# Three normalisations per half step: split in SBUF and turned by DMA instead of TensorE, two PSUM rings, the A and C layers swapped, and the loops written out

## What is computed

```
x = x + 0.5 * ffn(layernorm(x))          # layer A
x = x + ssm(layernorm(x))                # layer B (the names of the reference call it attention)
x = x + 0.5 * ffn(layernorm(x))          # layer C, the same weights as A

ffn: h = silu(x @ wg.T) * (x @ wu.T); h @ wd.T          # 256 -> 768 -> 256, int weights / 127
ssm: x_in, z = split(x @ in_w.T)                        # 256 -> 2 x 512
     xc = causal conv of 4 taps over x_in + bias
     dt_r, Bm = xc @ x_proj.T;  delta = clip(softplus(dt_r @ dt_w.T + dt_b), 0.001, 0.1)
     h = scan over tokens of exp(delta*A) * h + (exp(delta*A) - 1) / A * Bm      # 128 states
     out = ((h @ C.T + xc * D) * silu(z)) @ out_w.T
```

## Time and profile before

| what | us |
|---|---|
| median of three runs | 574.49 |
| lowest and highest run | 569.34, 575.93 |
| the profiled execution | 570.68 |
| its span | 568.8 |
| PE busy | 511.2 (90%) |
| DVE busy | 439.5 (77%) |

### The profile page before, as it was taken

The page is one execution under the profiler, slowest core; times in us unless marked ns, Lnnn a source line. Parts: engine busy times, 40 slices in busy tenths (PEclk is TensorE's granted clock), DMA queues, the critical chain, the costliest instruction groups (busy, mean ns, idle before and its releaser), DMA issues.

```text
span 568.8 us, 8689 instructions
## 1 busy us (share of the span) xinstructions
PE 511.2 (90%) x2705; PEld 297.9 (52%) x2705; DVE 439.5 (77%) x896; ACT 263.9 (46%) x449; POOL 227.5 (40%) x192
## 2 busy tenths in 40 slices
PE   3779978989999899888999899988999899998776
PEld 3346426636484357535484366535485366645434
DVE  5886897898768975798768986698868985797442
ACT  5374642456416471356506562355605563356032
POOL 2320246163623726053532817144441827153323
PEclk9969979999999999999999999999999999999979
DMA  9301000000200010000200011000200000000101
GB/s 303 89 1 39 2 0 2 0 2 3 75 2 1 1 61 17 3 2 2 75 2 1 1 39 39 3 2 1 76 2 1 1 20 21 1 1 3 37 1 38
DMA packets 14577, 13.80 MB, mean 24 GB/s; under 512 B 2592, under 2 KB 13856, under 8 KB 14512
## 3 DMA queue, kind: packets, MB, share of 16 engines
q1 hardware_dynamic: 13696, 12.12, 6.9%
q10 hardware_dynamic: 816, 0.79, 0.4%
HBM read 8.71 MB, written 4.19 MB: 23 GB/s over the span
## 4 chain that ended last, share of the span: by engine, by line
PE 31%; issue 30%; POOL 18%; DVE 17%; ACT 2%; DMA 1%; POOLq 1%; DVEq 0%; ACTq 0%
PE q L1259 17%; PE dp L1259 10%; POOL hl L418 6%; POOL xcl L425 4%; POOL yu L433 4%; DVE xn L706 3%; DVE h L728 3%; PE tp L1170 2%; DVE xc L756 2%; POOL rs_A L404 1%; POOL rs_C L404 1%; DVE yu L822 1%; DMA xpre<-in_L_attn_x_dram 1%; PE q L1170 1%; DVE xl L715 1%
## 5 line engine op out<-in xcount | busy, mean ns | idle before, releaser
L418 POOL TENSOR_TENSOR hl<-h,hh 128x512 f16<-128x512 f32 x96 | 119.2, 1249 | 111.1 <-ACT hh L548 110.1
L756 DVE SCALAR_TENSOR_TENSOR xc<-xi,cw,xc 128x512 f32<-128x512 f32 x96 | 93.5, 974 | 2.9
L728 DVE SCALAR_TENSOR_TENSOR h<-sg,hsm,q 128x512 f32<-128x512 f32 x96 | 70.7, 742 | 27.1 <-PE q L1259 14.4
L425 POOL TENSOR_TENSOR xcl<-xc,xch 128x512 f16<-128x512 f32 x32 | 43.9, 1383 | 90.2 <-ACT xch L563 90.2
L548 ACT ACTIVATE hh<-h 128x512 f16<-128x512 f32 x96 | 60.0, 625 | 42.1 <-DVE h L728 41.5
L533 ACT ACTIVATE xh<-tp 128x512 f16<-128x512 f32 x48 | 25.9, 592 | 114.5 <-PE tp L1170 114.1
L1259 PE MATMUL q<-xh,wu 128*128 128x512 f16 x192 | 57.8, 383 | 21.2 <-DVE h L728 19.3
L544 ACT ACTIVATE sg<-q 128x512 f32<-128x512 f32 x96 | 56.6, 589 | 28.3 <-PE q L1259 28.3
L1259 PE MATMUL dp<-wo,yu 128*128 128x256 f32 x256 | 58.6, 381 | 1.5 <-POOL yu L433 1.5
L1259 PE MATMUL q<-xh,wg 128*128 128x512 f16 x192 | 57.5, 381 | 2.6 <-DVE xl L715 2.0
L1259 PE MATMUL q<-xl,wg 128*128 128x512 f16 x192 | 57.8, 382 | 0.0
(11 more groups left out here) (177 smaller groups left out, 772.6 us busy)
## 6 DMA issues: line engine op xcount, KB each, us to landing
xpre<-in_L_attn_x_dram SPq DMA_DIRECT2D x8, 512.0 KB, 4.3
out_dram<-x SPq DMA_DIRECT2D x16, 256.0 KB, 2.2
xc<-in_L_attn_in_proj_w_dram SPq DMA_DIRECT2D x1, 1024.0 KB, 11.1
hl<-in_L_ffn_w_up_dram ACTq DMA_DIRECT2D x3, 256.0 KB, 5.9
hh<-in_L_ffn_w_gate_dram SPq DMA_DIRECT2D x3, 256.0 KB, 6.6
hh<-in_L_ffn_w_down_dram SPq DMA_DIRECT2D x1, 768.0 KB, 8.5
yu<-n_L_attn_out_proj_w_dram SPq DMA_DIRECT2D x1, 512.0 KB, 4.9
yu<-in_L_attn_x_proj_w_dram SPq DMA_DIRECT2D x1, 256.0 KB, 11.4
```

Of the source, the lines that this page charges most:

```text
L418: pool.tensor_tensor(HL[g.f][:, c, :], H[:, j, :], HH[g.f][:, c, :], ALU.subtract)\
L425: pool.tensor_tensor(XCL[:, m, :], XC[g.b][:, m, :], XCH[:, m, :], ALU.subtract)\
L728: dve.scalar_tensor_tensor(out=H[:, first % 3, :], in0=SG[:, first % 2, :], scalar=HSM[:, c:c + 1], in1=q[bank][:, :], op0=ALU.mult, op1=A ...
L756: dve.scalar_tensor_tensor(out=XC[s][:, m, :], in0=XI[s][:, m, k:k + TILE], scalar=CW[:, m, k:k + 1], in1=XC[s][:, m, :], op0=ALU.mult, op ...
```

## The change

- The turns on PE are gone, and so are `norm_lo` on DVE and the two tiles tp. `normalize` gives rows that are already scaled by 256 (the scale has gone into the variance). ACT rounds XN to f16 (`norm_hi`, two operations of 128x512), POOL subtracts for the low part (`norm_low`, two operations of 128x512), both beside each other in the tile XS16, and the SP queue issues two `dma_start_transpose` of 128x1024 f16 (256 KB each) from XS16 into XT. PE waits on their semaphore `turned` at `gu0` and at `ix`.
- XT is laid out by token block, so that a moving operand of 512 columns is four runs of 128 elements.
- The two freed PSUM banks become a ring of their own, sq (2 banks), for ix, iz, xp and cp. The ring q (4 banks) is for gate and up alone.
- In half steps 1 to 6 layer A comes first and C second: ix, iz, gate/up of A, xp, `down` A, gate/up of C, cp, `down` C, out. The norm of C has until after `down` A; A's norm for the next half step is made in the middle of this one. `skip_y` on DVE now comes after the residual of A, the statistics and the normalisation of Bnext and the last `h` of C. In half step 7 (B, C) and 8 (C) C is still the first layer. In half step 0, `gu1` of A has moved ahead of ix, and `down` A ahead of cp.
- Several tiles lose their second buffer (HH, HL, XC, SZ, YU), H gets a fourth. The loops are written out: no `Fori`, and every wait is for a constant.

The diff, cut to its core:

```diff
-RING = 4
+RINGS = {"g": 4, "s": 2}
+HID_BUFS = 4
...
 def tensor_order(h):
     if h == -1:
-        return [("fill", "early", -1), ("turn", "A", -1), ("fill", "up", -1), ("gu0", "A", -1),
-                ("gu1", "A", -1), ("turn", "A", 0), ("gu2", "A", -1), ("fill", "down", -1),
+        return [("fill", "early", -1), ("fill", "up", -1), ("gu0", "A", -1),
+                ("gu1", "A", -1), ("gu2", "A", -1), ("fill", "down", -1),
                 ("fill", "in", -1), ("fill", "delta", -1), ("down", "A", -1), ("fill", "late", -1),
-                ("gu0", "A", 0), ("turn", "Bnext", -1)]
+                ("gu0", "A", 0), ("gu1", "A", 0)]
+    steps = []
+    if has("B", h):
+        steps += [("ix", "B", h), ("iz", "B", h)]
+    steps += [(f"gu{n}", layers(h)[0], h) for n in range(2 if h == 0 else 0, 3)]
+    if has("B", h):
+        steps += [("xp", "B", h)]
+    steps += [("down", layers(h)[0], h)]
+    steps += [(f"gu{n}", part, h) for part in layers(h)[1:] for n in range(3)]
+    if has("B", h):
+        steps += [("cp", "B", h)]
+    steps += [("down", part, h) for part in layers(h)[1:]]
+    if has("B", h):
+        steps += [("out0", "B", h), ("out1", "B", h), ("out2", "B", h)]
+    return steps
...
+            def turn(g, k):                                   # SP
+                xt = XT.get((k, g.h), XT[k])
+                for j in range(2):
+                    sp.wait_ge(xn_lo, 2 * g.number("norm", k) + j + 1)
+                    sp.dma_start_transpose(
+                        xt[:, 2 * j:2 * j + 2, :, :, :].rearrange("p b w k t -> p (b w k) t"),
+                        XS16[:, 2 * j:2 * j + 2, :, :].rearrange("p b w d -> p (b w d)")).then_inc(turned, 16)
...
+            def norm_low(g, k):                               # POOL
+                for j in range(2):
+                    pool.wait_ge(xn_hi, 2 * g.number("norm", k) + j + 1)
+                    pool.tensor_tensor(XS16[:, 2 * j:2 * j + 2, 1, :], XN[:, 2 * j:2 * j + 2, :],
+                                       XS16[:, 2 * j:2 * j + 2, 0, :], ALU.subtract).then_inc(xn_lo, 1)
...
             def norm_hi(g, k):                                # ACT
-                for kc in range(KD):
-                    act.wait_ge(t_full[kc], g.number("turn", k) + 1)
-                    act.activation(XH[g.f][:, kc, :], tp[kc][:, :], ACT.Copy, scale=XS).then_inc(t_hi[kc], 1)
+                for j in range(2):
+                    act.wait_ge(xn_ready, 2 * g.number("norm", k) + j + 1)
+                    if j == 0:
+                        wait(act, turned, 32 * g.number("norm", k))
+                    act.activation(XS16[:, 2 * j:2 * j + 2, 0, :], XN[:, 2 * j:2 * j + 2, :], ACT.Copy)\
+                        .then_inc(xn_hi, 1)
...
             def half(g):                                      # ACT, new order
+                if B:
+                    conv_in(g); silu_z(g, (0,)); conv_high(g, (0,)); silu_z(g, (1,))
+                if C: norm_hi(g, "C")
+                if B: silu_z(g, (2, 3))
+                ...                                           # hid(0) ... hid(4, 5, 6), softplus, decay
+                if after.has("A"):
+                    norm_hi(after, "A")
+                if second:
+                    hidden(g, second, (0, 1, 2, 3))
+                if g.has("A"):
+                    norm_hi(g, "Bnext")
+                if second:
+                    hidden(g, second, (4, 5, 6))
...
             def half(g):                                      # DVE, new order after the last h of the first layer
+                    delta_in(g)
+                if after.has("A"):
+                    stats(after, "A", range(NB)); variance(after, "A")
+                if B:
+                    delta(g); series(g); coefficients(g); scan(g)
+                if after.has("A"):
+                    normalize(after, "A")
+                residual(g, one, 0)
+                if two: hidden(g, two, (0,))
+                residual(g, one, 1)
+                if two: hidden(g, two, (1,))
+                if A: stats(g, "Bnext", front); stats(g, "Bnext", rear)
+                if two: hidden(g, two, (2,))
+                if A: variance(g, "Bnext")
+                if two: hidden(g, two, (3,))
+                if A: normalize(g, "Bnext")
+                if two: hidden(g, two, (4, 5))
+                if B: skip_y(g)
+                if two: residual(g, two, 0); residual(g, two, 1)
+                if B: residual(g, "B", 0); stats(after, "C", front)
...
-            with pe.Fori(0, LOOPS) as i:
-                half(Half(1, i))
-                half(Half(2, i))
-            half(Half(LAST - 1))
-            half(Half(LAST))
+            for h in range(LAST + 1):
+                half(Half(h))
```

More of the change, by code:

```diff
@@ L455, in half @@
-                if g.has("C"):
-                    hidden_low(g, "C", range(HC - 2, HC))
-                if g.has("A") and g.h != 0:
-                    hidden_low(g, "A")
-                if g.has("B"):
-                    gate_y(g)
+                B, C, after = g.has("B"), g.has("C"), Half(g.h + 1)
+                first, second = (layers(g.h) + [None])[:2]
+                low = (lambda *c: hidden_low(g, first, c)) if g.h else (lambda *c: None)
+                if C:
+                    root(g, "C")
@@ L473, in _ @@
+                if second:
+                    hidden_low(g, second, (3, 4, 5))
+                if B:
+                    gate_y(g)
+            hidden_low(Half(-1), "A", (0, 1))
+            norm_low(Half(0), "A")
+            hidden_low(Half(-1), "A", (2, 3, 4, 5))
+            root(Half(-1), "Bnext")
+            norm_low(Half(-1), "Bnext")
+            hidden_low(Half(0), "A", (0, 1, 2, 3))
+            for h in range(LAST + 1):
+                half(Half(h))
         @block.scalar
@@ L1017, in _ @@
             weight_flag(0)
-            norm_lo(first, "A")
             hidden_scales()
@@ L1058, in _ @@
             normalize(first, "Bnext")
-            hidden(second, "A", (0, 1))
-            norm_lo(first, "Bnext")
+            hidden(second, "A", (0, 1, 2, 3))
             x_proj_unscale()
@@ L1112, in half @@
                         decay_finish()
+                if after.has("A"):
+                    stats(after, "A", range(NB))
+                    variance(after, "A")
+                if B:
                     delta(g)
[L1114 to L1116 removed]
                     series(g)
[L1118 to L1120 removed]
                     coefficients(g)
[L1122 to L1123 removed]
@@ L1136, in half @@
+                if A:
+                    normalize(g, "Bnext")
+                if two:
+                    hidden(g, two, (4, 5))
                 if B:
                     skip_y(g)
-                if A:
-                    for j in range(2):
-                        residual(g, "A", j)
-                        stats(g, "Bnext", (front, rear)[j])
-                    variance(g, "Bnext")
-                    normalize(g, "Bnext")
+                if two:
+                    residual(g, two, 0)
+                    residual(g, two, 1)
@@ L1161, in _ @@
-            half(Half(LAST - 1))
-            half(Half(LAST))
+                    stats(after, "C", front)
+            for h in range(LAST + 1):
+                half(Half(h))
         @block.tensor
```

540 lines of the change are left out of this document (237 added, 303 removed).

## The result

The changed kernel takes **610.98 us** (median of 4 runs, 608.53 to 613.33), the kernel before 571.92 (4 runs, three of them the ones behind the 574.49): a ratio of 1.068, 95% interval 1.059 to 1.077. The forecast was 588 with a range of 566 to 604: the sign was right, the size was not. The profiled execution spans 606.7 us against 568.8, 37.9 more.

A forecast was written before the change was run, and what follows sets the result against it. PE was taken to set the pace, DVE where convolution meets gate/up. On the 574.5 us median, -8.4 (six steady half steps), +4.9, +7.0, +6.8 and +3.5 (start and ends) gave 588.2 us, range 566 to 604.

The forecast's parts named there:

- The transposes' price: DMA transposes of normalised tiles: 3 us each to land, hidden in steady half steps, open at the ends.
- The moving operand of four runs: PE's products reading XT: four runs instead of one were booked at no cost.
- The writing out: Inner loop borders of the six steady half steps: removing them saves 1.1 us each, 6.6 in all.
- The first layer: Convolution and gate/up of A: POOL beside DVE costs 0.8 us (0 to 2), fourth `h` at 22.2, stall 2.4.
- The second layer: Gate/up of C and C projection: new stall of 3.4 us (1 to 5), third `cp` product waiting for `skip_y`.
- the clock in the steady half steps: Nothing booked in the six middle half steps; a lower clock, 2 us, was booked in half steps 0 and 7.
- Half step -1: Start: transposes land by 21, Bnext's norm is turned at 61.0, so half step 0 starts 4.9 us later.
- Half steps 0, 7 and 8: Ends, where transpose latency lies open: +7.0, +6.8 and +3.5 us.
- The 8 us idle before `cp` in half step 0: PE was to idle 8 us after `down` A until the later scan feeds `cp`.
- The rivals: Alternatives: DVE keeps up, 561 us (0.15); half the stall, 578 (0.25); slow transposes, 710 (0.10); worse ends, up to 600 (0.08).
- The ends are worse: Half steps 0, 7 and 8: low clock holds longer or unlooped instructions arrive late, up to 600 us; chance 0.08.
- the last sentence of the prediction: Signs of error: `skip_y` starts early, DVE beside POOL loses much more than 0.8 us, or a transpose takes long.

The follow-up runs named there:

- e4: Changed kernel, but PE's products of normalised tiles read one constant tile and wait for the low part, not the transposes, which still run: 594.45 us.
- e11: Changed kernel, but POOL's six norm operations per half step write only 4 of 256 columns each, order and waits kept: 598.65 us.
- e2: Changed kernel, but in half steps 1 to 6 POOL subtracts C's low part behind the first layer's fourth low part: 630.21 us.
- e5: Changed kernel with C's low part late, and SyncE issuing the next x load ahead of C's transposes: 600.61 us.
- e3: Changed kernel, but in half steps 1 to 6 Bnext is normalised, rounded and subtracted behind the last hidden chunks, skip product and gating: 595.95 us.
- e12: Changed kernel with its six product banks in one ring in program order, instead of four for gate/up and two for the attention: 596.09 us.
- e15: Changed kernel, but SyncE issues the first two transposes ahead of its last six weight loads: 605.63 us.
- e1: Kernel before with its loops written out and nothing else changed: 568.07 us.
- e7: Kernel before, written out, old layer order, one four-bank ring; only C's and A's norms of half steps 1 to 7 turned by DMA: 576.05 us.
- e8: Kernel before, written out, old layer order, with all norms turned by DMA, Bnext's and those at the ends too: 617.75 us.

## Why the prediction was wrong, point by point

- **The transposes' price: right.** 3.2 to 3.3 us to landing, 1.3 per issue; in half steps 2 to 6 they cost nothing (e4). By the Trainium skill, page "VectorE: DVE Perf Modes", section The three transpose paths, 1309 ns for a block of 128x128, a norm of 16 blocks would have taken 21 us (an estimate); the trace disagrees, with 3.2 us for each of the two transposes of 8 blocks. The moving operand of four runs costs nothing: 24 products of `in_proj` start 0.216 us apart as before.
- **The writing out: right.** 7.0 us where 6.6 stood.
- **"The first layer", the term for POOL beside DVE: the step that failed.** I took 0.8 us (0 to 2) from the means of two rows; it measured 3.5. The fourth `h` ended at 24.1 instead of 22.2, and the stall came to 4.3 instead of 2.4, 11.4 us in six half steps. A mean over 32 operations hid that DVE and POOL take turns operation by operation where they meet. e11 takes `norm_low`'s work away and gets the stall back to 3.0; e2 and e5 move C's part of it and get the same. That is 1.4 of the 1.9 us; the last 0.5 was not taken apart, and `conv_low` beside DVE is still in it.
  The Trainium skill, page "SBUF — State Buffer", section Who interferes with whom, says it: a DVE operation with two SBUF inputs contends with a GpSimd operation that reads SBUF, and where a DVE operation in a two-port mode, which tensor_scalar can enter, meets one, the second waits for the whole of the first. The trace agrees: four normalisations (tensor_scalar) last 5.20 us beside four gatings of 1.26, the taps with two SBUF inputs take 1.5 to 1.7 beside a POOL operation instead of 0.75, and `h` with one stays at 0.73. Priced by whole operations, the four DVE operations of conv 1 beside four of POOL (1.25 each) would have lasted at least 5.0 us instead of 2.8, and at most the sum of both, 7.8: an estimate of 2.2 to 5.0 us more, not 0.8.
- **"The second layer": right in kind, 4.2 instead of 3.4,** inside its bounds of 1 to 5. The wait stands where I put it, before the third C projection, released by `skip_y`. Bnext's normalisation, booked at 1.3, took 2.21 beside a `hl`: the same term again. The wait has more than one cause. Bnext's norm and rounding behind `skip_y` end all of it (e3); one ring of six alone takes 0.8 of the 3.0 and leaves a wait for the fifth `sg`, which stands behind ACT's rounding of Bnext (e12). That rounding was never moved by itself.
- **No term for the clock in the steady half steps.** Two of six took 1.7 us more behind a 3 us wait (3.3 in all). I had booked it for the ends only the earlier trace rows. e5 has the same wait in five half steps and none of this loss, e11 has a loss in three of five, so the 3.3 can't be laid to the order alone.
- **"Half step -1": wrong by 7.0.** I let the late first product (21, in truth 23.52) vanish in PE's slack and counted Bnext's chain alone. e4 and e15 show that the start has no such slack: 7.9 us earlier there (15.62) gives 7.0 at `in_proj`, and 4.6 gives 4.1. Of the 11.9 us, 7.0 are the transposes' latency, and issuing them ahead of six weight loads gives 4.1 back. I also had no term for `gu1` of A, which now stands ahead of `ix`: with the turns gone it leaves 2.3 of the 3.2 us by which e4 starts later than e1. The last 1.7 are what e1 itself starts later than the kernel before.
- **Half steps 0, 7 and 8: right in sum,** 6.2 and 10.4 against 7.0 and 10.3, and the second of them partly by luck: half step 7 gave 5.3 instead of 6.8, the wait ahead of half step 8 3.9 instead of 3.5, and the longer stretch of slow products behind it 1.1 where nothing stood. The 8 us idle before `cp` in half step 0 were 3.4; x_proj had waited 3.8 before.
- **The rivals.** None was it. "The ends are worse" named the low clock and late instructions, not a start without slack, and no rival was built on POOL beside DVE, though the last sentence of the prediction names it as what would make me wrong.

The misses add up: 11.4 (first stall), 3.2 (second: 0.8 in five half steps and 0.8 less in the sixth), 3.3 (clock), 7.0 (start) and -0.8 + 0.1 at the ends make 24.2; the spans differ by 37.9 - 13.8 = 24.1.

Open: why the clock falls behind a 3.02 us wait in some half steps and not in others of the same trace; what the last 0.9 of the 3.2 us are by which e4 starts half step 0 later (61.0) than the written-out kernel before (57.8); and why that kernel starts it 1.7 later than the looped one.

## What to carry to other kernels

Work moved to GpSimd is not free because GpSimd is idle: lay its operations beside those of VectorE in the timeline, and price each VectorE operation that meets one at a whole GpSimd operation (here the normalisations and the taps with two inputs from SBUF; `h`, with one from PSUM, was not held up). When a transfer moves behind another on an issuing queue, look who waits for the ones behind it; twice here an in-order queue took time: 4.1 us of the start, and 5.3 us of half step 2 in my second experiment (70.1, against 64.8 with the x load first). And a design is judged with its ring: the same transposes were level with the old kernel with four banks (574.55) and 2.5% faster with six (560.70), though the old kernel with six and no transposes was not run.

## What the runs showed of the hardware

- DVE beside POOL: four normalisations of 1.38 us together took 2.20 beside one POOL operation (e11), 3.04 beside two (e7), 5.20 beside four (e3). `h`, with one operand from PSUM, took 0.73 beside one, as alone.
- A DMA transpose of 256 KB of f16 within SBUF lands after 3.2 us, a plain store of the same size after 2.2.
- Two transposes issued right behind the last weight loads took 4.06 us to issue, with six loads fewer ahead of them 2.72 (e15).
- Waits of the same length, 3.02 us, were followed by a fall of the granted clock in two half steps of the five that have such a wait (0.97 instead of 1.00, 1.7 us lost), in e11 in three of five, and in e5 in none of five (3.01). In e8, behind 3.48 us, `in_proj` took 12.3 us instead of 10.4.
